# Weighting gathered table rows on ScalarE instead of VectorE, with five row buffers and fewer step increments

## What is computed

```python
q = (x @ Wq_pk).reshape(b, n, P, HEADS, DIM_KEY).transpose(2, 0, 1, 3, 4)
sim = jnp.einsum('pbnhd,pkhd->pbnhk', q, pk_keys)
scores, idx = jax.lax.top_k(sim, PK_TOPK)
...
score = (scores[0][..., :, None] + scores[1][..., None, :]).reshape(b, n, HEADS, PK_TOPK * PK_TOPK)
final_scores, pk_idx = jax.lax.top_k(score, FINAL_TOPK)
final_indices = jnp.take_along_axis(index, pk_idx, axis=-1)
final_scores = jax.nn.softmax(final_scores, axis=-1)
```

## Time and profile before

| | us |
|---|---|
| median of 3 runs | 8031.6 (8023.4 to 8049.1) |
| profiled execution, its own time | 8025.5 |
| its span | 8023.7 |
| busy: DVE | 4595.9 (57%) |
| busy: POOL | 4827.4 (60%) |
| busy: PE | 2931.5 (37%) |
| busy: ACT | 1275.6 (16%) |

### The profile page before, as it was taken

One profiled execution on the slowest core, in us unless ns is written; L12 is line 12 of the kernel. 1 busy time (PEld: TensorE's weight loads), 2 busy tenths in 40 slices (PEclk: granted clock), 3 DMA queues, 4 the chain that ended last, 5 costly groups with the idle time before them and its releaser, 6 DMA issues.

```text
span 8023.7 us, 45668 instructions
## 1 busy us (share of the span) xinstructions
PE 2931.5 (37%) x9994; PEld 1845.3 (23%) x9994; DVE 4595.9 (57%) x12390; ACT 1275.6 (16%) x2443; POOL 4827.4 (60%) x4418
## 2 busy tenths in 40 slices
PE   3569989711101223222322232232232222331227
PEld 1237664300000112111211121122121111121116
DVE  4667764456655657465746565665665465555522
ACT  1246653210000001000100010110101010010002
POOL 4225440037777677677766676777677667767761
PEclk7568886555555555555555555555555555555555
DMA  1000002111112111211121112112111211111110
GB/s 23 11 5 4 5 10 81 73 38 46 44 45 63 43 45 45 59 45 46 45 60 43 44 44 58 45 45 54 48 45 45 62 40 44 45 42 49 44 44 13
DMA packets 202945, 339.08 MB, mean 42 GB/s; under 512 B 117359, under 2 KB 117940, under 8 KB 202688
## 3 DMA queue, kind: packets, MB, share of 16 engines
q0 software_dynamic: 135168, 272.90, 13.4%
q1 hardware_dynamic: 67520, 63.39, 2.4%
HBM read 305.60 MB, written 30.43 MB: 42 GB/s over the span
## 4 chain that ended last, share of the span: by engine, by line
DVE 39%; another core or an unknown queue 17%; issue 16%; POOL 5%; PE 3%; ACT 1%; DMA 0%; DVEq 0%; SPq 0%; POOLq 0%; ACTq 0%
DVE sq_kv L2058 9%; DVE sq_rows L2051 6%; POOL sq_rows L1713 5%; DVE sq_is_cand L2004 3%; DVE sq_row_f L2006 3%; DVE sq_is_cand L2002 3%; DVE sq_d_negmax L1916 2%; DVE sq_top_at L1969 1%; DVE sq_top_at L1978 1%; DVE sq_sim_rest L1968 1%; DVE sq_c_negmax L2067 1%; DVE sq_top L1975 1%; DVE sq_top L1965 1%; DVE sq_d_diag L1918 1%
## 5 line engine op out<-in xcount | busy, mean ns | idle before, releaser
L1713 POOL DMA_INDIRECT sq_rows<-in_L_ffn_table,sq_row x4096 | 4351.1, 1062 | 1993.6 <-issue 1245.2
L1741 PE MATMUL sq_ps_d<-sq_d_q,sq_d_k 64*128 64x512 f32 x512 | 506.6, 1130 | 1789.6 <-ACT sq_exp_out L1850 985.5
L2058 DVE TENSOR_REDUCE sq_kv<-sq_rows 128x128 f32<-128x2048 f32 x256 | 916.9, 3582 | 226.0 <-remote 173.6
L1850 ACT ACTIVATE sq_exp_out<-sq_ps_d,sq_d_bias 128x512 f32<-128x512 f32 x256 | 175.9, 687 | 3296.0 <-DVE sq_d_bias L1919 2340.2
L2051 DVE TENSOR_TENSOR sq_rows<-sq_rows,sq_weight 128x2048 f32<-128x2048 f32 x256 | 584.3, 2283 | 152.9 <-DMA sq_rows<-in_L_ffn_table,sq_row 133.5
L1741 PEld LDWEIGHTS sq_ps_d<-sq_d_q,sq_d_k 64*128 64x128 f32 x512 | 126.2, 309 | 1958.4 <-ACT sq_exp_out L1850 1066.4
L952 POOL TENSOR_TENSOR at_psum_p<-at_prob 128x1024 f32<-128x1024 f32 x128 | 301.7, 2357 | 317.2 <-ACT at_prob L903 313.8
L1752 PE MATMUL sq_ps_c<-sq_kT,sq_qT 64*128 64x128 f32 (+2 forms) x384 | 225.4, 689 | 667.5 <-ACT sq_prob L1856 349.2
L1770 PE MATMUL sq_ps_o<-sq_kv,sq_probT 128*128 128x64 f32 x1280 | 306.3, 405 | 320.5 <-DVE sq_y L2082 166.9
L1856 ACT ACTIVATE sq_prob<-sq_ps_c,sq_c_negmax 128x128 f32<-128x128 f32 (+3 forms) x256 | 134.9, 527 | 1721.0 <-DVE sq_c_negmax L2067 847.2
L1770 PEld LDWEIGHTS sq_ps_o<-sq_kv,sq_probT 128*128 128x128 f32 x1280 | 301.7, 332 | 338.5 <-issue 338.2
(11 more groups left out here) (345 smaller groups left out, 6387.4 us busy)
## 6 DMA issues: line engine op xcount, KB each, us to landing
sq_rows<-in_L_ffn_table,sq_row POOLq DMA_INDIRECT x4096
qkvT<-exp_rows SPq DMA_DIRECT2D x32, 768.0 KB, 3.3
sq_d_q<-qkvT SPq DMA_DIRECT2D x8, 1024.0 KB
sq_d_k<-qkvT SPq DMA_DIRECT2D x8, 1024.0 KB
sq_d_v<-qkvT SPq DMA_DIRECT2D x8, 1024.0 KB
tok_rows<-in_L_tok_hash_rows,tok_idx_now POOLq DMA_INDIRECT x128
tok_chars<-in_x SPq DMA_DIRECT2D x8, 128.0 KB
h<-tok_h_tok SPq DMA_DIRECT2D x8, 128.0 KB, 2.0
```

Source lines behind the costliest of these rows:

```text
L1713: pool.indirect_dma_start(rows[j % GSLOTS][:, k, :], None, w2["table"], bass.IndirectOffsetOnAxis(row[(4 * r.c + t) % 3][:, h, k:k + 1], 0 ...
L1741: pe.matmul(ps_d[u % 2][:, :], d_k[f, h // 2, t * P:(t + 1) * P], d_q[f, h // 2, :], start=True, stop=True).then_inc(S["d_scores"], 1)
L2058: s.did(dve.tensor_reduce(kv[r.par][:, t, :, h, :], slot[:, :, :].rearrange("p j (m c) -> p m c j", m=2), AX.X, ALU.add))
```

## The change

ScalarE multiplies each gathered row by its weight: 16 ACTIVATE Copy instructions per step, 128x128 each, with a per-token scale, the last thing in ACT's step. They wait for the gather, and raise `rows_weighted`. `weigh` leaves DVE. `add_rows` moves from the end of step j to the end of step j + 1 and waits for `rows_weighted`. `GSLOTS` is 5, and buffers are numbered through all rounds. Several increments of the step semaphore are merged: in the search functions only the last instruction of a loop carries one, and at a few places a step increment with a wait and a separate increment becomes one increment on the instruction.

```diff
-GSLOTS = 4
+GSLOTS = 5
...
+                        if r.mix and j < UN:
+                            if h == 0:
+                                act.wait_ge(S["weight_ready"], r.at(TT, t + 1))
+                            n = r.at(UN, j)
+                            act.wait_ge(gathered[n % GSLOTS], 16 * TOPK * (n // GSLOTS + 1))
+                            slot = rows[n % GSLOTS]
+                            for k in range(TOPK):
+                                ins = act.activation(slot[:, k, :], slot[:, k, :], ACT.Copy, scale=weight[(4 * r.c + t) % 3][:, h, k:k + 1])
+                            ins.then_inc(S["rows_weighted"], 1)
...
                 def best8(groups, values, at, source, rest):
 
                     for g in groups:
-                        s.did(dve.max(values[:, g, 0:8], source[:, g, :]))
+                        ins = dve.max(values[:, g, 0:8], source[:, g, :])
+                    s.did(ins)
                     s.wait()
                     for g in groups:
-                        s.did(dve.match_replace(rest[:, g, :], values[:, g, 0:8], source[:, g, :], LOW))
-                        s.did(dve.max_index(at[:, g, 0:8], values[:, g, 0:8], source[:, g, :]))
+                        dve.match_replace(rest[:, g, :], values[:, g, 0:8], source[:, g, :], LOW)
+                        ins = dve.max_index(at[:, g, 0:8], values[:, g, 0:8], source[:, g, :])
+                    s.did(ins)
...
-                def weigh(r, u):
-
-                    t, h = divmod(u, HEADS2)
-                    slot = rows[u % GSLOTS]
-                    dve.wait_ge(gathered[u % GSLOTS], r.at(16 * TOPK * UN // GSLOTS, 16 * TOPK * (u // GSLOTS + 1)))
-                    s.did(dve.tensor_tensor(slot[:, :, :], slot[:, :, :], bc(weight[(4 * r.c + t) % 3][:, h, :], 2, KV), ALU.mult))
-
                 def add_rows(r, u):
 
                     t, h = divmod(u, HEADS2)
-                    slot = rows[u % GSLOTS]
-                    s.wait()
-                    s.did(dve.tensor_reduce(kv[r.par][:, t, :, h, :], slot[:, :, :].rearrange("p j (m c) -> p m c j", m=2), AX.X, ALU.add))
-                    s.wait()
-                    dve.sem_inc(S["rows_used"], 1)
+                    slot = rows[r.at(UN, u) % GSLOTS]
+                    dve.wait_ge(S["rows_weighted"], r.at(UN, u + 1))
+                    dve.tensor_reduce(kv[r.par][:, t, :, h, :], slot[:, :, :].rearrange("p j (m c) -> p m c j", m=2), AX.X, ALU.add).then_inc(S["rows_used"], 1)
...
-                        if r.mix and j < UN:
-                            weigh(r, j)
                         if j < UN and r.chosen(t) and 2 * h + 1 < 14:
                             choose(r, t, 2 * h + 1)
-                        if r.mix and j < UN:
-                            add_rows(r, j)
+                        if r.mix and 1 <= j <= UN:
+                            add_rows(r, j - 1)
```

More of the change, by code:

```diff
@@ L1606, in sequence_pipeline @@
                  "moments_ready std_ready xn_ready f_ps f_used sim_ready sim_used best_centred weight_exp row_ready "
-                 "rows_used q_ready kv_ready c_in c_used c_scores c_max c_probs t_ps t_used o_ps o_used y_ready y_stored")
+                 "rows_used weight_ready rows_weighted q_ready kv_ready c_in c_used c_scores c_max c_probs t_ps t_used o_ps o_used y_ready y_stored")
         S = {n: sem(n) for n in names.split()}
@@ L1712, in body @@
                         for k in range(TOPK):
-                            pool.indirect_dma_start(rows[j % GSLOTS][:, k, :], None, w2["table"],
-                                                    bass.IndirectOffsetOnAxis(row[(4 * r.c + t) % 3][:, h, k:k + 1], 0)).then_inc(gathered[j % GSLOTS], 16)
+                            pool.indirect_dma_start(rows[r.at(UN, j) % GSLOTS][:, k, :], None, w2["table"],
+                                                    bass.IndirectOffsetOnAxis(row[(4 * r.c + t) % 3][:, h, k:k + 1], 0)).then_inc(gathered[r.at(UN, j) % GSLOTS], 16)
                 rounds(pool, body)
@@ L1949, in diagonal_tile @@
                     s.wait()
-                    s.did(dve.bn_aggr(moments[:, :], stats[:, :]))
-                    s.wait()
-                    dve.sem_inc(S["moments_ready"], 1)
+                    dve.bn_aggr(moments[:, :], stats[:, :]).then_inc(S["moments_ready"], 1)
+                    dve.wait_ge(S["moments_ready"], r.at(TT, TT + t + 1))
                     dve.wait_ge(S["std_ready"], r.at(TT, TT + t + 1))
@@ L1974, in next8 @@
                     for g in groups:
-                        s.did(dve.max(values[:, g, 8:16], rest[:, g, :]))
+                        ins = dve.max(values[:, g, 8:16], rest[:, g, :])
+                    s.did(ins)
                     s.wait()
                     for g in groups:
-                        s.did(dve.max_index(at[:, g, 8:16], values[:, g, 8:16], rest[:, g, :]))
+                        ins = dve.max_index(at[:, g, 8:16], values[:, g, 8:16], rest[:, g, :])
+                    s.did(ins)
                 def candidates():
@@ L1992, in candidates @@
                         for src, dst in ((top, cand), (top_at_f, cand_row)):
-                            s.did(dve.tensor_tensor(
+                            ins = dve.tensor_tensor(
                                 dst[:, :, at:at + na * nb].rearrange("p h (a b) -> p h a b", b=nb),
-                                bc(src[:, 0:HEADS2, a0:a1], 3, nb), bc(src[:, HEADS2:GROUPS, 0:nb], 2, na), ALU.add))
+                                bc(src[:, 0:HEADS2, a0:a1], 3, nb), bc(src[:, HEADS2:GROUPS, 0:nb], 2, na), ALU.add)
                         at += na * nb
+                    s.did(ins)
                     s.wait()
@@ L2034, in choose @@
                         s.wait()
-                        s.did(dve.tensor_copy(row[b][:, :, :], row_f[:, :, :]))
-                        s.wait()
-                        dve.sem_inc(S["row_ready"], 1)
+                        dve.tensor_copy(row[b][:, :, :], row_f[:, :, :]).then_inc(S["row_ready"], 1)
                         dve.wait_ge(S["weight_exp"], tile + 1)
```

14 lines of the change are left out of this document (5 added, 9 removed).

## The result

The changed kernel takes 8197.1 us (median of 4 runs, 8166.1 to 8203.5) where the kernel before takes 8027.5 us on the same chip: a ratio of 1.020, 95% interval 1.017 to 1.023. The profiled execution took 8203.5 us, its span is 8201.4 us.

A forecast was written before the change was run, and what follows sets the result against it. The prediction took the chain to run through VectorE (39%) and idle time around it (33%), with GpSimd close behind. From 8025.5 us, -584 + 34 + 60 + 3 gave 7538.5, plus 6 for the median: 7545 us, range 7160 to 7900.

The forecast's parts named there:

- The product leaves VectorE, -584 us: VectorE's line of work in each of 256 steps: 2.283 us less per step, taken whole as -584 us.
- The product leaves GpSimd alone, counted 0: GpSimd's gathers: 315 us cheaper without VectorE's product beside them, counted 0 since GpSimd was not the chain.
- ScalarE, 0 in a step: ScalarE's 16 products: 4.9 us a step, hidden behind VectorE's other 12 us of work, so 0.
- the prediction has 671: The sum if ScalarE's product, 4.9 us a step, lay on the path: +671 us and not -584.
- Fifth buffer 0, increments 0: Sum one step later with one more buffer: 0 in a step; fewer increments in searches and candidates: 0.
- Round ends, +60 us and +3 us: Last product and sum before the kv transposes, 7 rounds: +60 us; the end of the program: +3 us.
- the +34 us for steps that wait for gathers: The 15 steps where VectorE waits for a gather: it would only wait longer, 2.28 us each, +34 us.
- Rival A: Increments cause the slow stretches on VectorE; these go and GpSimd becomes the bound: 7178 us, chance 0.22.
- Rival B: Slow stretches last until VectorE is as far behind as before; only GpSimd's 315 us is saved: 7780 us, chance 0.22.
- Rival C: ScalarE falls under the same delay, its instructions 1.40 us apart in slow stretches: 8279 us, chance 0.10.
- The test I had set: First to last gather: the prediction is wrong if this stage is not between 5350 and 6000 us.

The follow-up runs named there:

- e4: The changed kernel without ScalarE's product, so the rows are added unweighted and VectorE waits for the gather itself: 8152.4 us, ratio 1.015.
- e10: The changed kernel with a useless product of the old size added on VectorE, on a scratch tile at the old place: 8026.9 us, ratio 0.998.
- e9: The kernel before, its VectorE product replaced by a sum of 10 of 16 rows with one SBUF input, about as long: 8324.0 us, ratio 1.037.
- e3: The changed kernel with four row buffers instead of five: 8191.3 us, ratio 1.020.
- e1: The kernel before with only the merged increments (searches, candidates and three tile-wise places): 8020.7 us, ratio 0.998.
- e2: The changed kernel with the old increments, one per instruction of a search: 8198.9 us, ratio 1.021.
- e18: The kernel of e12 run again on the chip of e16: 7768.4 us, ratio 0.955.
- e16: The changed kernel itself on another chip, where the kernel before takes 8124.6 us: 8183.9 us, ratio 1.007.
- e13: The changed kernel with gathered rows of 256 bytes instead of 512, as many gathers and row transfers: 8193.9 us, ratio 1.004.
- e12: The changed kernel with four buffers and a 128x192 memset on GpSimd after every gather: 7720.8 us, ratio 0.962.

## Why the prediction was wrong

*The product leaves VectorE, -584 us.* The size was right (604 us less busy), its effect was not. I took it whole because it stood on the chain. But much of the chain's other 33% was a delay whose size depends on GpSimd, and e4 shows the product gone from every engine with nothing gained.

*The product leaves GpSimd alone, counted 0.* This is the step that failed. The size was near: 315 us forecast, 389 us measured, the mean 0.967 and not 0.985 us. (One row had given 1.23 us for a product; the mean over all 256 is 1.52 us, and what is left for the 128x800 products is some 95 us and not 168.) But I asked only whether a faster GpSimd would be of use or would not, and wrote 0. Its sign was negative: a GpSimd that isn't held up issues 1.25 us apart for whole steps, and the delay grows. In its place the runs showed 162 us more of stage, with a wait of 876 us and not 226 at `c_inv`. e10 gives the hold back with 585 us of VectorE's work, and wins 2%. The rows said so beforehand: slow stretches ended when GpSimd stopped. I read that as a fact about the end of a stretch, not about its cause.

On the hold itself the runs are clear: a product with two SBUF inputs makes the mean gather 1.060 us (e10), a sum with one leaves it at 0.968 us (e9), and ScalarE on the same buffers leaves it at 0.967 us, against 0.965 us without it (e4). With that the trace agrees with the rule of the Trainium skill, SBUF — State Buffer, section "SBUF: two separate sides" (a VectorE operation with two SBUF inputs locks a port pair shared with GpSimd, and ScalarE waits on nobody's port), in both halves, the one on ScalarE's own ports too.

*ScalarE, 0 in a step.* Nearly right: 4.8 us for the sixteen against 4.9, and about 45 us on the time (e4). With ScalarE's product on the path the sum would have been +670 us (the prediction has 671), and that product costs next to nothing here. The rule of the Trainium skill, ScalarE: Activation LUTs, "Rules for kernel authors", is to multiply on VectorE and not on ScalarE. The trace agrees as to the engine's time (4.8 us against 2.28), but the change is slower for another reason.

*Fifth buffer 0, increments 0.* Right, by e3, and by e1 and e2. *Round ends, +60 us and +3 us*, and the +34 us for steps that wait for gathers, weren't measured alone; beside the failed step they are small.

*Rival A* (the increments, 7178 us) falls by e1. *Rival B* (the stalls come back, 7780 us) came nearest to the mechanism, and its sign showed: VectorE's idle time is larger than before. Its price was wrong, because I let the stretches last only until VectorE was as far behind as before. They go on until a buffer runs out, at every third head (92 waits in 256), and the delay reaches PE's results, some 20 us each. *Rival C* (8279 us), left outside the range, had nearly the right time for a wrong reason: the 16 ACTIVATEs are 0.30 us apart in a burst of 4.77 us, and ScalarE has 1% of the chain. The test I had set, a stage between 5350 and 6000 us, failed: 6377 us.

## What to carry to other kernels

When a chain holds much time that belongs to no engine, find out what turns that time on before subtracting work from the chain, and ask of each engine that becomes faster whether it drives it. A run of gathers issued back to back by GpSimd can be too fast: a short instruction between them kept GpSimd busy for 1124 us more and saved 416 us of the whole here (e18 against e16). Test a suspected hold or pace in both directions, by the same work without the hold (e9) and by the hold with useless work (e10); together they rule out that VectorE's busy time alone was the cause.

## What the runs showed of the hardware

- While 128-row gathers are issued 1.25 us apart, instructions of VectorE start 0.7 to 1.4 us apart instead of 0.1 to 0.2, a result of PE was taken 29.8 us after it was made (4781.2 to 4811.0 us) and one of VectorE by ScalarE 9.1 us after. About 5 us after the gathers pause it is over (5.3 us here). At 1.39 us apart most of the delay of PE's results is gone (189 us of waits and not 906, e18 and e16); the searches are still late, which costs little there. The bytes play no part (e13). What the resource is, no run shows.
- VectorE's products with two SBUF inputs, which cost the gathers 1.52 us each on average (389 us in 256), worked as a governor. A known conflict can be worth keeping until what it prevents is known.
- A memset between two gathers takes up half of the gap between them: 0.30 us become 0.16, so that 0.27 us of work cost 0.14 us (e12).
- The same kernel before takes 8028 to 8157 us by chip, the changed one 8197 and 8184. The sign of the change is the same on the two chips on which both were run, its size is not: 1.020 and 1.007.
